# Attention and linear attention on one core: the value products of a visit moved to the front of their tick

## The reference

```python
def _mha(q, k, v, Wq, bq, Wk, bk, Wv, bv, Wo, bo, gamma, beta):
    Q = (q @ Wq.T + bq).reshape(B, S, N_HEAD, D_K).transpose(0, 2, 1, 3)
    K = (k @ Wk.T + bk).reshape(B, S, N_HEAD, D_K).transpose(0, 2, 1, 3)
    V = (v @ Wv.T + bv).reshape(B, S, N_HEAD, D_K).transpose(0, 2, 1, 3)
    score = jnp.einsum('bhqd,bhkd->bhqk', Q, K) / jnp.sqrt(jnp.float32(D_K))
    att = jax.nn.softmax(score, axis=-1)
    out = jnp.einsum('bhqk,bhkd->bhqd', att, V)
    out = out.transpose(0, 2, 1, 3).reshape(B, S, D_MODEL)
    out = out @ Wo.T + bo
    x = out + q
    ...
def _L1_xattn_ref(query, key, value, gamma, beta):
    Q_phi = jax.nn.elu(query)
    K_phi = jax.nn.elu(key)
    KV = jnp.einsum('bnd,bne->bde', K_phi, value)
    Z = 1.0 / (jnp.einsum('bnd,bd->bn', Q_phi, K_phi.sum(axis=1)) + ATTN_EPS)
    attn = jnp.einsum('bnd,bde->bne', Q_phi, KV) * Z[..., None]
    x = query + attn
    ...
```

## Time and profile before

| | before |
|---|---|
| median of three runs | 1510.83 us |
| profiled execution, its span | 1509.6 us |
| TensorE busy | 1473.3 us (98%) |
| VectorE busy | 1227.3 us (81%) |
| GpSimd busy | 1206.0 us (80%) |
| ScalarE busy | 900.9 us (60%) |
| mean granted TensorE clock | 0.994 |

### The profile page before, as it was taken

How to read it: one execution, slowest core, us unless ns; L and a number is a source line. 1 busy time by engine, 2 the same in 40 slices (tenths; PEclk the granted TensorE clock), 3 DMA queues, 4 the chain that set the end, 5 groups by cost and what they waited for, 6 DMA issues and landing times.

```text
span 1509.6 us, 30353 instructions
## 1 busy us (share of the span) xinstructions
PE 1473.3 (98%) x10584; PEld 1038.6 (69%) x10584; DVE 1227.3 (81%) x2442; ACT 900.9 (60%) x1846; POOL 1206.0 (80%) x1031
## 2 busy tenths in 40 slices
PE   8999999999999999999999999999999999999996
PEld 6767767676766767667677767766767767766554
DVE  6687898878788788887779788898688978899865
ACT  3464655556666666665566665665566666566664
POOL 0487787867898898877789988887789888888964
PEclk9999999999999999999999999999999999999999
DMA  7745163443425225344343425424252442520001
GB/s 222 200 144 143 54 181 128 130 128 97 122 73 157 89 90 146 105 132 138 90 129 98 135 68 158 149 87 133 79 157 77 129 127 70 148 88 26 14 23 42
DMA packets 159575, 170.14 MB, mean 113 GB/s; under 512 B 20288, under 2 KB 122048, under 8 KB 159424
## 3 DMA queue, kind: packets, MB, share of 16 engines
q1 hardware_dynamic: 157696, 167.16, 37.4%
q10 hardware_dynamic: 1728, 1.05, 0.2%
HBM read 125.97 MB, written 42.21 MB: 111 GB/s over the span
## 4 chain that ended last, share of the span: by engine, by line
PE 85%; DVE 4%; DMA 3%; issue 3%; POOL 2%; ACT 2%; SPq 1%; POOLq 0%; ACTq 0%; DVEq 0%
PE score L471 15%; PE scoreT L485 14%; PE acc L503 14%; PE misc L565 7%; PE misc L542 7%; PE misc L553 7%; PE misc L590 7%; PE misc L529 6%; PE misc L582 5%; PE acc L519 2%; DVE maxes L810 1%; POOL pair_sum L1072 1%; DMA q_stack<-q_dram 1%; PE misc L573 1%; DVE pair_sum L850 1%
## 5 line engine op out<-in xcount | busy, mean ns | idle before, releaser
L657 ACT ACTIVATE p_ring<-scoreT 128x512 f32<-128x512 f32 x1024 | 594.2, 594 | 496.9 <-PE scoreT L485 493.6
L1072 POOL TENSOR_TENSOR pair_sum<-p_ring 128x512 f32<-128x512 f32 x504 | 665.5, 1329 | 173.9 <-ACT p_ring L657 111.5
L810 DVE TENSOR_REDUCE maxes<-score 128x1 f32<-128x512 f32 x1024 | 677.3, 679 | 151.2 <-PE score L471 146.0
L471 PE MATMUL score<-k_stack,q_stack 96*128 96x512 f32 x1024 | 599.5, 587 | 5.4 <-DVE maxes L810 2.1
L485 PEld LDWEIGHTS scoreT<-q_stack,k_stack 104*128 104x128 f32 x2048 | 387.7, 191 | 156.7 <-ACT p_ring L657 81.6
L485 PE MATMUL scoreT<-q_stack,k_stack 104*128 104x256 f32 x2048 | 419.7, 287 | 7.3 <-ACT p_ring L657 5.1
L471 PEld LDWEIGHTS score<-k_stack,q_stack 96*128 96x128 f32 x1024 | 193.1, 189 | 161.5 <-issue 106.6
L503 PE MATMUL acc<-p_ring,v_sb 128*32 128x256 f32 x4096 | 249.9, 385 | 0.0
L1081 POOL TENSOR_TENSOR pair_sum<-pair_sum 128x512 f32<-128x512 f32 x189 | 248.8, 1316 | 0.0
L850 DVE TENSOR_TENSOR pair_sum<-pair_sum 128x512 f32<-128x512 f32 x189 | 197.2, 1043 | 1.9 <-POOL pair_sum L1072 1.7
L503 PEld LDWEIGHTS acc<-p_ring,v_sb 128*32 128x32 f32 x4096 | 120.6, 110 | 85.3 <-issue 3.2
(11 more groups left out here) (112 smaller groups left out, 1373.9 us busy)
## 6 DMA issues: line engine op xcount, KB each, us to landing
xT_sb<-xT_in SPq DMA_DIRECT2D x63, 512.0 KB, 3.8
q_stack<-q_dram SPq DMA_DIRECT2D x189, 128.0 KB, 2.6
k_stack<-k_dram SPq DMA_DIRECT2D x93, 256.0 KB, 4.7
ctx_nat<-ctx_in SPq DMA_DIRECT2D x32, 256.0 KB, 4.7
q_dram<-q_high SPq DMA_DIRECT2D x63, 128.0 KB, 1.9
q_dram<-q_low SPq DMA_DIRECT2D x63, 128.0 KB, 2.1
k_dram<-k_high SPq DMA_DIRECT2D x31, 256.0 KB, 2.0
k_dram<-k_low SPq DMA_DIRECT2D x31, 256.0 KB, 2.2
```

The lines of the kernel that those rows point to most:

```text
L471: pe.matmul(score[k % 3][:], q_stack[0:SPLIT, unit % NQ, j, t * P:(t + 1) * P], k_stack[0:SPLIT, group_of[unit] % 2 * QUAD + j, h * HALF:( ...
L657: act.activation(p_ring[:, n % NP, h * HALF:(h + 1) * HALF], scoreT[k % 2][:], ACT.Exp, scale=SCALE).then_inc(A["exped"], 1)
L810: dve.reduce_max(maxes[:, unit % 2, t, j, h:h + 1], score[k % 3][:], AX.X).then_inc(V["maxed"], 1)
L1072: pool.tensor_tensor(pair_sum[:, place_of_pair(pair), cols], p_ring[:, (n - 1) % NP, cols], p_ring[:, n % NP, cols], ALU.add).then_inc(L[" ...
```

## The change

In TensorE's loop over the ticks the call of `visit` goes from the end of the tick to its front. Nothing else changes; the planner's tables, all waits and the other engines' programs are the same.

```diff
             for k in range(FIRST, LAST):
+                if visiting(k) is not None:
+                    visit(visiting(k))
                 if 0 <= k < HALVES:
                     pass1(k)
                 if 0 <= k - LEAD < HALVES:
                     pass2(k - LEAD)
                 beside(k)
-                if visiting(k) is not None:
-                    visit(visiting(k))
```

## The result

The changed kernel takes 1528.16 us (median of four runs, 1525.61 to 1531.38); the kernel before 1511.21 in the same comparison. The ratio is 1.0111, 95% interval 1.0092 to 1.0130: **slower by 1.1%**, some 17 us. The profiled execution is the slowest of the four (its span is 1529.8 us), so its trace shows 20 us against the trace of before. The four executions took 1525.61, 1527.28, 1529.05 and 1531.38 us at a mean granted clock of 0.994, 0.993, 0.992 and 0.991; the profiled execution of the kernel before had 0.994. At that same clock the distance is some 15 us (1525.61 against 1510.83); the rest of the 17 to 20 goes with the clock.

The account below looks back on a forecast made before the run. TensorE, busy 98% of 1509.6 us, was taken to bound the kernel, so only its waits could change. Terms 0 - 3.5 + 4.4 + 1.7 = +2.6 us on 1510.83 gave 1513.4 us, range 1509.0 to 1518.0.

Parts of the forecast that it names:

- no measurable change: Whole kernel: a difference within about 0.2% (3.0 us), what a measurement can tell; chance 52%.
- Change of place by itself: 0: TensorE going into and out of the visit (V): no dearer from a side product than from turned-score products; 0 us.
- What V no longer stands behind: -3.5: Waits of a visit's tick's score and turned-score products now pass under the visit (V): 3.5 us gained.
- What V now waits for: +4.4: Sums (L519) at a unit's last visit (V) start 0.47 us sooner and wait for pair-sum adds: 4.4 us lost.
- What now starts after V: +1.7: VectorE's maximum, ScalarE's exponentials and work queued with them start after the visit (V), delaying later products: 1.7 us lost.
- Bounds: 0 and 1.9 a visit: Limits for work now starting after the visit: 0, or 1.9 us a visit if ScalarE and VectorE had no slack.
- clock rival: Waiting bare pairs of ticks behind visits drop two more stretches to low clock: 3.2 us more, 1516.6; chance 8%.
- pair-sum rival: Sums (L519) at units' last visits become a steady wait: +5.5 us, 1516.3; chance 24%.
- sign named for "right": TensorE's score products: waits of L471 for VectorE's maxima (L810) would fall from 2.1 us.
- One named for "wrong": TensorE's clock: more stretches at the low clock would show the forecast wrong.

Follow-up runs that it names:

- run 1: The changed kernel with only the four sum products (L519) moved back to the tick's end; ratio 1.0139 against the kernel before, +21 us.
- run 11: The kernel before with the sums (L519) one tick later, behind p2(k+1), the next tick's turned-score products; ratio 1.0097, +15 us.
- run 2: The changed kernel with the visit between the tick's score product and its turned-score products; ratio 1.0013 against the kernel before, +2 us.
- run 6: The changed kernel with row maxima over 256 of 512 keys; ratio 0.9990 against the kernel before, where the old order with such maxima had 0.9972.
- run 9: The changed kernel with VectorE's maximum behind the other work of a visit's tick; ratio 1.0055 against the kernel before, +8 us.
- run 12: The kernel before with only first visits moved to the front, maximum and exponentials there behind their tick's other work; ratio 1.0013, +2 us.
- run 3: The changed kernel with turned-score products, then visit, then score product, pass2 ahead of pass1 in all ticks; ratio 1.0126 against the kernel before, +19 us.
- run 10: The kernel before, old order, with every visit planned one tick earlier; ratio 1.0227, +34 us.

## Why the prediction was wrong

It said 1513.4 us, within 1509.0 to 1518.0, and held "no measurable change" for likeliest. The sign it leant to was right; the size was not.

**"Change of place by itself: 0"** was right. In the changed kernel the visit starts 0.52 us after the last product of L542, L565, L590 or L595 (128x512) in all 55 visits that follow one; such products follow each other after 0.43, so going in costs 0.09, as in the one case of the earlier trace rows. The shortest distances sum to the same. The rule that a change of tiling mode drains TensorE (the Trainium skill, TensorEngine Tiling (Array Packing), Key Properties) fits the 0.33 us that an extra pair of changes costs in runs 1 and 11, though no trace shows that a drain is the reason. The cost does not depend on what stands ahead, and the change adds none. (One count was off: 124 visits stand in a tick with a p1, not 123.)

**"What V no longer stands behind: -3.5"** was right: -3.6.

**"What V now waits for: +4.4"** was right in kind and somewhat small: +5.8, and the sums wait in 16 units where 12 had too little room by my count. Added to it is a wait I had excluded. I wrote that a visit's start conditions were met more than 1 us before; with the change the last step of `normalise`, L875, ends only 0.10 us ahead of three visits, because VectorE is later:

```profile
442.67 0.41 DVE L875 TENSOR_TENSOR outT<-acc,den_rows 128x256 f32<-128x256 f32 x1
...
443.18 0.64 PE L503 MATMUL acc<-p_ring,v_sb 128*32 128x256 f32 x8 [0.59 <-issue]
```

**"What now starts after V: +1.7"** is the step that failed. The starts show 3.9 at p1, 1.9 at p2, 3.2 at side products and 1.8 at visits, 10.8 us, and a part of the sums' wait. Two things were wrong in how I reckoned it. I carried each visit's delay forward only on VectorE and ScalarE, and looked for it only where p1 and p2 wait; side products wait for VectorE too, and so do the sums, the next visit, ScalarE and GpSimd, and each hands it on. And I let idle time take the delay up against the times of the old trace, one visit at a time, as if VectorE's 146.0 us of idle time for scores were there to be used. Most of it (85 of the 146.0 us) stood ahead of max(k) or of the maximum right behind a visit, which is where the change makes it useless: VectorE's idle time for scores grew by 42 us, and all its idle time by 27, while its work stayed. Runs 2, 6, 9 and 12 show this cause from four sides; run 3 agrees, with the reserve named there, and run 10 stays unexplained.

**"Bounds: 0 and 1.9 a visit"** held the truth, 0.1 us a visit, but the range was not built from them. I put the value near the lower end because of the idle totals, and then gave the range only 0.5 us for it.

The clock rival, with 8%, is there on top of it: I had reckoned two more stretches at the low clock and 3.2 us, and the trace has 10 us more at the low level, some 5 us. Most of that lies behind the last visit, not behind bare pairs after a visit as I had put it, and kernels in the old order meet it too, so in this part the distance is chance. The pair-sum rival, at 1516.3, named a mechanism that is there and is a third of the loss. One sign named for "right" failed, the telling one: the waits of L471 for L810 rose from 2.1 to 5.5 us where they should have fallen. One named for "wrong" came: more time at the low clock.

## What to carry to other kernels

A long block on the busiest engine that needs nothing fresh is cover for the others. Place it where they have just been handed work, not ahead of handing it over: the same block at the front of a step starved VectorE here for its length, and at 81% busy, with its lag at its greatest just there, it did not get that back. An engine's idle total says nothing of slack until one has seen when the idle time falls; where it falls under the very block that is moved, it is no reserve. A quick test before such a change: make the suspected engine's work smaller, and see if the order still matters; compare the granted clocks of the two before you read a few microseconds.

## What the runs showed of the hardware

Each change between products over all 128 columns and products of 32 columns side by side has its price in whatever place: 0.1 us more going in, and some 0.2 coming out. Four small products taken away from the sixteen that they stood beside cost 0.33 us in each of 63 places, so that run 11 is 15 us slower with a wait less. I had reckoned 0.2 us a place there, and nothing in run 1.

The four executions of the changed kernel differ by 5.8 us with the same instructions, and each 0.001 less of mean granted clock goes with 1.9 us more.
